# Token mixer: value and denominator rounds issued in three pairs instead of six single rounds, and the first attention tile projected inside the last mixer tile

## The reference

```python
def _L0_tok_ref(qkv):                       # 128 sequences, 3*32 channels, 512 positions
    ch = qkv.shape[1] // 3
    q, k, v = jnp.split(qkv, 3, axis=1)
    scale = 1.0 / np.sqrt(np.sqrt(ch))
    weight = jnp.einsum('bct,bcs->bts', q * scale, k * scale)
    weight = jax.nn.softmax(weight.astype(jnp.float32), axis=-1).astype(weight.dtype)
    return jnp.einsum('bts,bcs->bct', weight, v)

h = _L0_tok_ref(x)
h = h + _L0_attn_ref(_layernorm(h), wq, wk, wv, wo)      # causal attention, 32 heads of 16, rope
h = h + _L0_ffn_ref(_layernorm(h), w1, w3, w2)           # ternary weights
h = h + _L1_attn_ref(_layernorm(h), Wq, Wk, Wv, Wo)
h = h + _L1_ffn_ref(_layernorm(h), gate_up_packed, ...)  # 4-bit weights
```

## Time and profile before

| | |
|---|---|
| runs | 2330.85, 2330.91, 2333.66 us; median 2330.91 |
| the profiled execution | 2331.95 us, of which the span of the profile is 2330.2 |
| token mixer in full swing | from 27 us to 531 us, one tile every 15.8 us |
| TensorE busy | 2189.6 us (94% of the span) |
| VectorE busy | 1677.4 us (72%) |
| ScalarE busy | 1520.1 us (65%) |
| GpSimd busy | 1267.9 us (54%) |

### The profile page before, as it was taken

How to read it: one execution, slowest core, us unless ns; L and a number is a source line. 1 busy time by engine, 2 the same in 40 slices (tenths; PEclk the granted TensorE clock), 3 DMA queues, 4 the chain that set the end, 5 groups by cost and what they waited for, 6 DMA issues and landing times. The chain is left out here.

```text
span 2330.2 us, 42739 instructions
## 1 busy us (share of the span) xinstructions
PE 2189.6 (94%) x13828; PEld 1074.8 (46%) x13828; DVE 1677.4 (72%) x2922; ACT 1520.1 (65%) x2430; POOL 1267.9 (54%) x1141
## 2 busy tenths in 40 slices
PE   6899999987999998899999999999998999999997
PEld 1222222224666665444444444666664444444443
DVE  7777777775788988656667633666666788788775
ACT  4566666666688787446565424677665777777775
POOL 4566667667777778223234301444454566666654
PEclk9999999999999999999999999999999999999999
DMA  5444445441244221312223212222221011111111
GB/s 145 134 134 138 129 136 138 127 125 60 89 130 132 70 68 65 101 48 80 77 91 97 69 50 69 79 80 81 81 82 41 23 51 50 41 50 42 43 36 64
DMA packets 144050, 195.00 MB, mean 84 GB/s; under 512 B 30469, under 2 KB 73957, under 8 KB 143898
## 3 DMA queue, kind: packets, MB, share of 16 engines
q1 hardware_dynamic: 111642, 154.52, 21.8%
q10 hardware_dynamic: 32256, 38.54, 5.7%
HBM read 125.10 MB, written 42.21 MB: 72 GB/s over the span
## 5 line engine op out<-in xcount | busy, mean ns | idle before, releaser
L2293 PE MATMUL f_bank<-f_xs,gu 128*128 128x512 f16 x1408 | 417.0, 379 | 1.6 <-ACT f_firstg L2119 1.1
L371 DVE TENSOR_REDUCE tm_negmax<-tm_s 128x1 f32<-128x512 f32 x512 | 325.5, 682 | 90.7 <-PE tm_s L426 88.4
L321 ACT ACTIVATE tm_prob<-tm_s 128x1024 f32<-128x1024 f32 x256 | 258.6, 1025 | 192.7 <-PE tm_s L446 192.7
L2321 PE MATMUL f_bank<-dn,f_ghi 128*128 128x512 f16 x704 | 265.5, 379 | 1.9 <-DVE f_glo L2228 1.9
L274 POOL TENSOR_TENSOR tm_added<-tm_prob 128x1024 f32<-128x1024 f32 x96 | 224.6, 2354 | 33.8 <-ACT tm_prob L321 33.4
L2083 POOL TENSOR_TENSOR f_firstg<-f_firstg,f_secondg 128x512 f32<-128x512 f32 x88 | 152.4, 1731 | 152.7 <-DVE f_secondg L2212 152.7
L426 PE MATMUL tm_s<-tm_qk 96*128 96x512 f16 x512 | 200.8, 395 | 31.9 <-DVE tm_negmax L371 17.8
L446 PE MATMUL tm_s<-tm_qk 98*128 98x512 f16 x512 | 196.2, 386 | 32.2 <-ACT tm_prob L321 27.3
L2293 PEld LDWEIGHTS f_bank<-f_xs,gu 128*128 128x128 f16 x1408 | 135.9, 98 | 162.8 <-ACT f_firstg L2119 1.5
L2083 POOL TENSOR_TENSOR f_firstu<-f_firstu,f_secondu 128x512 f32<-128x512 f32 x88 | 123.9, 1408 | 64.3 <-DVE f_secondu L2212 64.2
L1048 PE MATMUL a_bankB<-a_wo,a_yThi 128*128 128x512 f16 x512 | 157.1, 389 | 0.0
(11 more groups left out here) (197 smaller groups left out, 5792.5 us busy)
## 6 DMA issues: line engine op xcount, KB each, us to landing
tm_qk<-tm_xs SPq DMA_DIRECT2D x384, 64.0 KB, 2.3
tm_xqk<-in_qk ACTq DMA_DIRECT2D x32, 512.0 KB, 4.7
a_hin<-h SPq DMA_DIRECT2D x64, 256.0 KB, 2.7
a_hres<-h SPq DMA_DIRECT2D x64, 256.0 KB, 3.1
h<-a_hout SPq DMA_DIRECT2D x64, 256.0 KB, 2.5
f_hin<-h SPq DMA_DIRECT2D x64, 256.0 KB, 2.9
f_hres<-h SPq DMA_DIRECT2D x64, 256.0 KB, 2.9
tm_vt<-in_vt ACTq DMA_DIRECT2D x32, 256.0 KB, 2.9
```

What stands on the lines that cost most here:

```text
L321: nc.scalar.activation(prob[b][:, 2 * h:2 * h + 2, :], s2[:, i % 2, :, :], ACT.Exp, scale=SCALE).then_inc(exp_done, 1)
L371: nc.vector.tensor_reduce(negmax[u][:, m:m + 1], s1[:, BANK[p], :], AX.X, ALU.max, negate=True).then_inc(s1_read, 1)
L2293: last = nc.tensor.matmul(bank_of(m, i)[:, :], (gate, up)[which][:, j, m * P:(m + 1) * P], xs[g % 2][:, x, j, :], start=x == 0, stop=x == 1)
L2321: last = nc.tensor.matmul(pz[i][:, :], gparts[x][:, (MT * g + m) % RING, i * P:(i + 1) * P], down[w][:, m, :], start=m == 0 and c % 3 == 0 ...
```

## The change

Six things are changed in the mixer and three around it.

1. `VALUES_AT` and `SUMS_AT`: values j = 0 and 1 both in slot 14 of their own tile, j = 2 and 3 both in slot 4 of the next, both rounds with ones in slot 9.
2. `BANK` and the marks around the sums: the stretch with two banks moves from blocks 5 to 12 (as placed in `BANK`) to blocks 8 to 15.
3. GpSimd: `normalise` goes behind the two adds of a step.
4. ScalarE: the copy of the denominators goes from behind exponential 3 to behind 4, `x_hi` from 4 to 5, the store of the rows from behind exponential 5 of step n (tile n - 2) to behind exponential 0 (tile n - 3).
5. VectorE: `inverse_sums` goes from slot 14 to slot 1 of the step after.
6. SP: the turned maxima go ahead of the two transfers of the inverse denominators, which both are for tile n - 2.
7. The hook `between` lets attention steps run within mixer step 31: on TensorE x(0) is turned in slot 4 and x(1) turned and tile 0 projected in slot 13; ScalarE and VectorE take their part within the step; ScalarE copies the projection behind exponential 7.
8. On SP and GpSimd the attention's step -3 goes ahead of mixer step 31.
9. The inversion of the last tiles' denominators is shifted by one step.

```diff
@@ token_mixer
-    BANK = (1, 2, 0, 1, 2, 0, 1, 0, 1, 0, 1, 0, 1, 2, 0, 1, 2, 0)
-    SUMS_BANK, FIRST_BEHIND_SUMS = 2, 13
+    BANK = (1, 2, 0, 1, 2, 0, 1, 2, 0, 1, 0, 1, 0, 1, 0, 1, 2, 0)
+    SUMS_BANK, LAST_BEFORE_SUMS, FIRST_BEHIND_SUMS = 2, 7, 16
-    VALUES_AT = {14: (0, 0), 0: (1, 1), 2: (1, 2), 4: (1, 3)}
-    SUMS_AT = {5: 0, 7: 1}
+    VALUES_AT = {14: (0, (0, 1)), 4: (1, (2, 3))}
+    SUMS_AT = {9: (0, 1)}
@@ sync
             stack(n + 1, 1 - u, 2)
+            maxima(n, u, 1)
+            inverses(n - 2, u, k - 1)
+            stack(n + 1, 1 - u, 3)
             inverse_rows(n - 2, u, k - 1)
-            maxima(n, u, 1)
-            stack(n + 1, 1 - u, 3)
             stack(n + 2, u, 0)
             maxima(n + 1, 1 - u, 0)
             stack(n + 2, u, 1)
-            inverses(n - 1, 1 - u, k + u - 1)
@@ gpsimd
             add(n - 1, 2)
+            add(n, 0)
+            add(n, 1)
             if not isinstance(n, int) or n < TILES:
                 normalise(n - 2, u, k - 1)
-            add(n, 0)
-            add(n, 1)
             x_lo(n + 3, 1 - u)
@@ scalar
                     load_values(n + 1, 1 - u)
-                if i == 3:
+                if i == 0:
+                    store(n - 3, 1 - u)
+                if i == 4:
                     copy_sums(n - 1, 1 - u)
                     denominators(n - 1, 1 - u)
-                if i == 4:
+                if i == 5:
                     x_hi(n + 3, 1 - u, k + 1 + u)
-                if i == 5:
                     load(n + 4, u)
-                    store(n - 2, u)
+                if between is not None:
+                    between(i)
@@ vector
+                if g == 1:
+                    inverse_sums(n - 2, u, k - 1)
                 if g == 2:
                     add_last(n - 1)
-                if g == 14:
-                    inverse_sums(n - 1, 1 - u, k + u - 1)
+                if between is not None:
+                    between(g)
@@ tensor
-                        wait(pe, s1_read, use(t + 2, 4) + 1)
+                        wait(pe, s1_read, use(t + 2, LAST_BEFORE_SUMS) + 1)
...
-                behind, j = VALUES_AT.get(g, (0, None))
-                if j is not None:
+                behind, blocks = VALUES_AT.get(g, (0, ()))
+                for j in blocks:
                     sum_values(n - behind, (u + behind) % 2, k - behind + (u and behind), j)
                 if g in SUMS_AT and not (isinstance(n, int) and n == TILES):
-                    sum_probs(n - 1, SUMS_AT[g])
-                if isinstance(n, int) and n == TILES - 1 and g == SLOTS - 1:
+                    for j in SUMS_AT[g]:
+                        sum_probs(n - 1, j)
+                if isinstance(n, int) and n == TILES - 1 and g == 12:
                     pe.wait_ge(sums_out, n)
@@ mixer_into_attention, scalar
+            if i == 2:
+                run(step, -3, -3)
+            if i == 7:
+                copy_projected(0, 0)
@@ mixer_into_attention, tensor
-        run(mix, 28, 31)
-        prepare(BEGIN)
-        run(step, -3, -3)
+        run(mix, 28, 30)
+
+        def between(g):
+            if g == 4:
+                prepare(BEGIN)
+                run(step, -3, -3)
+            if g == 13:
+                run(step, -2, -2)
+
+        mix(31 // 2, 1, between)
         run(mix, 32, 32)
-        run(step, -2, -2)
         sum_probs(31, 0)
         sum_probs(31, 1)
```

More of the change, by code:

```diff
@@ L343, in denominators, with step @@
                     .then_inc(dens_in[u], 16)
-        def step(k, u):
+        def step(k, u, between=None):
             n = 2 * k + u
@@ L842, in step @@
             copy_kT(n + 1)
-            if rope:
+            if rope and n + 2:
                 copy_q(n + 2, u)
@@ L848, in step @@
                 copy_q(n + 2, u)
-            copy_kv(n + 2, u)
+            if not rope or n + 2:
+                copy_kv(n + 2, u)
             probs_hi(n)
@@ L856, in step @@
                 later(n + 3 - TILES)
-        return prepare, step
+        return prepare, step, copy_projected
     def vector(dve):
@@ L1164, in _ @@
         run(step, -4, -4)
-        run(mix, 30, 31)
-        run(step, -3, 0)
+        run(mix, 30, 30)
+        run(step, -3, -3)
+        run(mix, 31, 31)
+        run(step, -2, 0)
         run(mix, 32, 32)
@@ L1195, in _ @@
         prepare(BEGIN)
-        run(step, -5, -4)
+        run(step, -5, -3)
         run(mix, 31, 31)
-        run(step, -3, -3)
         run(mix, 32, 32)
@@ L1214, in _ @@
     def _(act):
-        mix, copy_values, copy_sums, denominators = mixer.scalar(act)
-        prepare, step = att.scalar(act)
+        mix, store, copy_values, copy_sums, denominators = mixer.scalar(act)
+        prepare, step, copy_projected = att.scalar(act)
         run(mix, -4, -1)
@@ L1229, in _, with between @@
         run(mix, 30, 30)
-        prepare(WO)
         prepare(BEGIN)
         run(step, -5, -4)
-        run(mix, 31, 31)
-        run(step, -3, -3)
+        prepare(WO)
+        def between(i):
+            if i == 2:
[3 more added lines that the diff above has]
+        mix(31 // 2, 1, between)
+        store(29, 1)
         copy_values(31, 1, 15)
@@ L1259, in _ @@
         run(step, -4, -4)
-        run(mix, 31, 31)
-        run(step, -3, -3)
+        def between(g):
+            if g == 6:
+                run(step, -3, -3)
+        mix(31 // 2, 1, between)
         add_last(31)
         run(step, -2, 0)
-        inverse_sums(31, 1, 15)
+        inverse_sums(30, 0, 15)
         statistics, normalised, low, _, _ = ternary.vector(dve)
```

11 lines of the change are left out of this document (9 added, 2 removed).

## The result

The changed kernel takes **2429.16 us** (median of four runs, 2405.88 to 2435.43) against 2331.38 before. The ratio, taken over all single runs and not from these two medians, is 1.0403, with a 95% interval from 1.0343 to 1.0462: 4% slower, some 94 us. The forecast had the sign and one of two mechanisms, and half the size: +49 us, where the medians lie 98 apart. 2429 us is above its range of 2316 to 2388, and above the collision's own range of 2366 to 2390.

What follows compares the result with a forecast made beforehand. No mixer engine is full, so waits that go round set the time. +51 us (collision, tiles 2 to 28) + 1 (tiles 0 and 1) - 3 (passage) = +49 on 2331.95; median forecast 2380 us, range 2316 to 2388.

Steps and rivals of the forecast that it cites:

- the sign: Whole kernel: slower than before, chance 0.66, against 0.25 for faster and 0.09 for the same.
- the collision's own range: Whole kernel if the adds collide: 2366 to 2390 us, from 1.4 to 2.1 us a tile and the passage's ends.
- The collision term: Mixer tiles 2 to 28: VectorE's fourth `added` waits for GpSimd's third add, 17.7 us instead of 15.80, +51 us; chance 0.64.
- The margin: Mixer tile: GpSimd's third add begins 0.3 to 0.4 us ahead of VectorE's arrival at its fourth `added`.
- Where TensorE stops: Mixer tile: TensorE's slot 9 waits for VectorE to free a bank, until 15.29 us after the tile's t = 0.
- the sum: Whole kernel: +51 for tiles 2 to 28, +1 for tiles 0 and 1, -3 for the passage, +49 us.
- the passage term: Mixer to attention: 6.3 us saved up to the first turned q, tile 31 longer by 3.3, gain 3 (1 to 6).
- rivals 1 and 2: Mixer tile: no harmful collision, 15.5 to 15.9 us, 2325, chance 0.22; or VectorE comes first, 15.4 us, 2317, chance 0.11.
- Rival 3: Mixer tile: TensorE decides, the pairs save 0.75 us a tile, 2308 us; chance 0.03.

Runs made afterwards that it cites:

- e1: Changed kernel, but GpSimd's third add of a tile also waits until VectorE's fourth `added` is done; 2347.00 us, 1.0060 to the kernel before.
- e9: Changed kernel with seven repeated score blocks on TensorE ahead of the block where it waits 1.47 us, tiles 4 to 27; 2396.80 us, 1.0261.
- e2: Changed kernel with the passage to attention of the kernel before, collision kept; 2426.96 us, 1.0367 to the kernel before.
- e5: e1 with three VectorE reductions that nobody reads behind the fourth `added`, a delay in place of the collision; 2414.31 us, 1.0340.
- e6: Kernel before, single rounds, with four VectorE reductions that nobody reads behind `added`; 2425.55 us, 1.0387.
- e3: Changed kernel with e1's wait on GpSimd and the passage to attention of the kernel before; 2343.39 us, 1.0043.
- e4: Kernel before with the changed passage to attention alone, cast of wo moved behind attention's first steps; 2338.78 us, 1.0019.
- e7: e4 with ScalarE's cast of wo ahead of attention's first steps again; 2335.47 us, 1.0010.
- e8: e3 with GpSimd's low parts of the weights and ScalarE's cast of wo moved from ahead of tile 31's exponentials; 2341.63 us, 1.0034.
- e10: Kernel before with one pair of values: values 2 and 3 both in slot 4, nothing in slot 2; 2341.10 us, 1.0026.
- e11: Kernel before with both rounds with ones in slot 7, slot 5 empty; 2336.65 us, 1.0010.
- e12: Kernel before with the edits of e10 and e11 together; 2341.96 us, 1.0032.

## Why the prediction was half right

- **The collision term was right, for three tiles too many.** Forecast: GpSimd ahead by 0.3 to 0.4 us, VectorE held until t + 10.53, next block at 11.54, 17.7 us a tile. Measured: ahead by 0.19, held until 10.56, next block at 11.57, 17.69. 1.88 us a tile were forecast, 1.89 measured, and in e1, without the collision, the tile is 0.18 shorter than before. The margin was half of mine, in part since the reciprocal held VectorE for only 0.15 us. But I counted tiles 2 to 28, 51 us, and the adds met in tiles 4 to 27: 24 x 1.89 = 45. The rule that the Trainium skill gives in SBUF — State Buffer, section "SBUF: two separate sides", that the second of the two waits for the whole of the first, agrees with every tile of the changed kernel in which these adds meet: VectorE waits in tiles 4 to 27, and GpSimd (3.36 us instead of 2.37) in tile 2, where VectorE came first by 0.06 us. A margin of 0.19 us decided this, half of one that the forecast itself held to be small: that the sign came out right is in part luck.
- **Where TensorE stops was wrong in place, not in sum.** I let it stop in slot 9. It stops at slot 6 for 1.47 us and then for 0.59 and 0.33, because VectorE's delay shows as soon as TensorE has no free bank left.
- **The first step that failed is one that I did not take: the sum had no term for TensorE's clock.** The earlier trace rows have it at 1.00; the prediction does not speak of it, and so took full clock for a loop in which TensorE was to stop for 2 us more in every tile. By e9 against the changed kernel that is 1.0403 - 1.0261, some 33 us; by the rows, 12.2 us in the profiled run and 37.2 in e2's. The Trainium skill (TensorE: Matmul & The Clock Gate, section "HAM oscillation — how this bites in real kernels") describes a loop that falls back to half clock because TensorE waits between its blocks. The traces agree in kind; the case told there is one of long waits for data, and here stops of which the longest was 1.47 us were enough. Neither of the other causes that I had, pairs or lock, is needed for the clock to fall (e5, e6).
- **The second step that failed: the passage term had the wrong sign.** I took a gain of 3 us. What I had counted as the gain is there: 8.2 us from the last score block (602.42) to the first turned q (610.64) instead of 14.1. But I let tile 31 grow by 3.3 us, and it grew by 11.9 (from 59.7 behind at its start to 71.6 at the last score block). The projection of tile 0 and the turning of x(1) stand in it in full, 4.3 us (595.88 to 600.22). 5.0 are the stop of 6.96 us instead of 1.99: 1.8 of them are the passage's, by the cast of wo (6.97 in e1 against 5.17 in e3, 3.78 in e4 against 1.98 in e7), and 3.2 are the loop's, as e3 has them with the old passage. The prediction does not name the cast and so put it at nothing; it had been hidden in the wait, and now stands behind it. The rest came with half clock, 0.72 in the mean from 578 to 596 us (pair of values 3.65 instead of 1.95). In e4, alone on the old loop, the changed passage costs 0.19%, 4.4 us; by e1 against e3 3.6, which is within the noise of those two.
- **The rest** is some 10 us that e3 has over the kernel before, though its tiles are 0.18 shorter (15.62 us, as rivals 1 and 2 had it). My two rivals without a collision gave 2325 and 2317; they too lacked the clock, and the longer stop of tile 31. By the score blocks of its trace e3 is level at the start of tile 4, loses 1.3 us there, where the clock falls (0.93 in the mean from 75 to 100), is 2.4 ahead at the start of tile 29 and 0.4 ahead at that of tile 31. It is 5.2 behind at the last score block (3.2 by the stop; clock 0.66 from 520 to 530), 3.7 at the first copy of q, 10.8 at the sixth (0.77 from 550 to 575) and 11.3 at the end. So the loss lies in tiles 29 to 31 and in attention's first tiles. Why the clock falls in the latter is open. From 550 to 575 it is 0.77 in e3, 0.86 in e8, but also 0.83 in e4 and 0.87 in e10, which do not have the new order; it is 1.00 in e7, e11 and the kernel before. TensorE's three long stops there are nearly the same in the kernel before (2.85, 2.96 and 2.02 us) and in e3 (2.86, 3.32 and 2.01). With one trace of each kernel I can't tell an effect of the order from one of the single execution.
- **Rival 3, TensorE's 0.75 us a tile**, had the least chance and rightly: e1 shows 0.18 without the collision, and e10 to e12 show less than nothing for one or two pairs. My reading that TensorE "runs without a stop through slots 14 to 8" was true, but it was no sign that TensorE set the pace: it ran level with VectorE.

In the measured ratios: 4.0% = 1.4 the clock in the loop (e9), 2.0 the collision (e9 to e1), 0.2 the passage (e1 to e3), 0.4 what the new order costs besides (e3). Against the forecast, some 45 us are missing (94 - 49): 33 by the clock in the loop, 7 by the passage (-3 forecast, +4 in e4), and 5 as the balance of what e3 lost besides and of the three tiles too many.

## What to carry to other kernels

Where a change lengthens TensorE's stops in a loop that ran at full clock, the forecast needs a term for the clock, and one run with the stop filled by repeated matmuls tells how large it is. Two engines whose SBUF adds pass each other within a few tenths of a microsecond should be ordered by a semaphore on the side that has slack; here one such wait was worth some 80 us, as it took away the stop and with it the falls of the clock. Before work is moved out of a place, ask what it was hidden behind there, on its own engine and on the one that it keeps pace with: neither the cast of wo nor the single rounds cost anything where they stood.

## What the hardware showed that I had not expected

- Half clock comes and goes within a loop that is otherwise regular: in the changed kernel's profiled run in every third tile for some 3 us at a cost of 1.5 us, in e2's run in most tiles, up to 2.36 us each, with one and the same order of work. The same program has runs of 2406 and of 2432 us, which fits; of the changed kernel only the faster run has a trace, and e2, whose loop is the same, shows the other kind; e9, whose clock holds in the loop, has runs within 3.4 us of each other.
- A lock of 2.07 us and a plain delay of 1.85 us in the same place differ by about their length: 17.69 and 17.40 us a tile.
